# Routing an MoE layer in three groups beside the attention part, in one block, with the router on rows before the layer norm

## What is computed

```python
x = x + xattn(layernorm(x), side, ctx)      # two SmoothQuant int8 products a batch
x = x + ffn(layernorm(x), router_w, gate_proj, up_proj, down_proj)
```

## Time and profile before

| what | us |
|---|---|
| median of 3 runs (420.90 to 422.14) | 421.02 |
| profiled execution | 421.27 |
| its span, first to last instruction | 419.4 |
| PE busy | 322.5 (77%) |
| POOL busy | 246.4 (59%) |
| ACT busy | 209.7 (50%) |
| DVE busy | 209.2 (50%) |

### The profile page before, as it was taken

One profiled execution on the slowest core, in us unless ns is written; L12 is line 12 of the kernel. 1 busy time (PEld: TensorE's weight loads), 2 busy tenths in 40 slices (PEclk: granted clock), 3 DMA queues, 4 the chain that ended last, 5 costly groups with the idle time before them and its releaser, 6 DMA issues.

```text
span 419.4 us, 5809 instructions
## 1 busy us (share of the span) xinstructions
PE 322.5 (77%) x1712; PEld 202.4 (48%) x1738; DVE 209.2 (50%) x442; ACT 209.7 (50%) x378; POOL 246.4 (59%) x260
## 2 busy tenths in 40 slices
PE   0638758879887678861166999999999999999960
PEld 0525445567656446651143555555555555555530
DVE  2584899887898855500871333333333333323310
ACT  1558559878779767453101444444444444444430
POOL 2484698677869565458304265666566656656440
PEclk9957966995899795865555999999999999999996
DMA  7936406693178347035004266766666666675552
GB/s 258 314 115 216 161 41 203 192 358 100 26 253 325 109 144 275 27 125 225 1 0 127 36 117 102 131 112 115 120 125 106 116 110 125 106 134 102 90 70 27
DMA packets 26667, 57.00 MB, mean 136 GB/s; under 512 B 2576, under 2 KB 12816, under 8 KB 24592
## 3 DMA queue, kind: packets, MB, share of 16 engines
q0 software_dynamic: 8816, 20.71, 27.5%
q1 hardware_dynamic: 17824, 35.93, 24.6%
HBM read 37.50 MB, written 19.14 MB: 135 GB/s over the span
## 4 chain that ended last, share of the span: by engine, by line
issue 27%; POOL 12%; PE 8%; POOLq 2%; DMA 1%; ACT 0%; DVE 0%; SPq 0%
POOL xg L772 8%; PE bank_r L1007 4%; PE bank_h L1029 3%; POOLq L778 2%; POOL out L782 1%; DMA xg<-tokens,gather_at 1%; POOL hold_p L198 1%; POOL number L754 1%; PE bank_t L995 1%; PE bank_q L1018 0%; POOL out L757 0%; ACT y L953 0%; DVE aT L900 0%; ACT aT L948 0%; POOL no_later L764 0%
## 5 line engine op out<-in xcount | busy, mean ns | idle before, releaser
L1007 PE MATMUL bank_r<-gu_hi,xT 128*128 x312 | 107.0, 385 | 1.0 <-DVE xT L891 0.2
L782 POOL DMA_INDIRECT out<-y,scatter_at x39 | 61.7, 1583 | 51.2 <-ACT y L953 50.0
L891 DVE SCALAR_TENSOR_TENSOR xT<-bank_t,xT 128x512 f16<-128x512 f32 x39 | 27.0, 691 | 66.3 <-ACT xT L933 66.3
L772 POOL DMA_INDIRECT xg<-tokens,gather_at x39 | 38.5, 986 | 29.1 <-DVE gather_at L881 17.3
L1007 PE MATMUL bank_r<-gu_lo,xT 128*128 x144 | 55.1, 383 | 0.0
L1029 PE MATMUL bank_h<-dn_hi,aT 128*128 x156 | 52.8, 379 | 1.7 <-DVE aT L900 1.4
L953 ACT ACTIVATE y<-bank_h,slot_weight 128x512 f32<-128x512 f32 x39 | 26.8, 687 | 36.8 <-PE bank_h L1029 36.8
L1007 PEld LDWEIGHTS bank_r<-gu_hi,xT 128*128 128x128 f16 x312 | 30.8, 99 | 29.5 <-issue 2.5
L360 POOL TENSOR_TENSOR gu_lo<-stage,gu_hi 128x1024 bf16<-128x1024 f32 x16 | 34.0, 2129 | 13.1 <-ACT gu_hi L578 13.0
L933 ACT ACTIVATE xT<-bank_t 128x512 f16<-128x512 f32 x39 | 23.0, 589 | 24.8 <-PE bank_t L995 24.7
L906 DVE SCALAR_TENSOR_TENSOR gated<-bank_r,gated 128x256 f32<-128x256 f32 x39 | 16.6, 425 | 37.3 <-ACT gated L941 37.3
(11 more groups left out here) (156 smaller groups left out, 629.7 us busy)
## 6 DMA issues: line engine op xcount, KB each, us to landing
x_in<-in_x SPq DMA_DIRECT2D x4, 1024.0 KB, 5.4
w_in<-in_fside_BxS2xS SPq DMA_DIRECT2D x4, 1024.0 KB, 6.3
stage<-in_L_ffn_gate_proj SPq DMA_DIRECT2D x8, 512.0 KB, 4.9
stage<-in_L_ffn_up_proj SPq DMA_DIRECT2D x8, 512.0 KB, 3.7
stage<-in_L_ffn_down_proj SPq DMA_DIRECT2D x8, 512.0 KB, 4.8
x<-in_x SPq DMA_DIRECT2D x4, 1024.0 KB, 6.2
out<-x SPq DMA_DIRECT2D x4, 1024.0 KB, 6.7
tokens<-xn SPq DMA_DIRECT2D x4, 1024.0 KB, 6.4
```

The costliest lines, as they stand in the source:

```text
L772: pool.indirect_dma_start(out=xg[:, i % XG], out_offset=None, in_=tokens_dram, in_offset=bass.IndirectOffsetOnAxis(ap=gather_at[:, i:i + 1 ...
L782: pool.indirect_dma_start(out=out, out_offset=bass.IndirectOffsetOnAxis(ap=scatter_at[:, i:i + 1], axis=0), in_=y[:, i], in_offset=None, c ...
L891: dve.scalar_tensor_tensor(out=xT[i % 2][:, 1].rearrange("p c t -> p (c t)"), in0=bank_x[:, i % 2], scalar=X_SCALE, in1=xT[i % 2][:, 0].re ...
L1007: ins = pe.matmul(bank_gu[:, i % 2], xT[i % 2][:, part, c], rhs[:, cols], start=(c == 0 and n == 0), stop=(c == C - 1 and n == 2))
```

## The change

The second block is gone: its steps stand at the ends of the same five lists. The routing is cut in three groups, batches 0 and 1, batch 2 and batch 3. For each group there is "choose" (the two best scores, DVE), "place" (ranks on PE, then DVE gives each row a slot; each expert owns 16 tiles of 128 slots, so that a group's places don't depend on later groups), and "table" (one-hot products on PE summed into a table of 128 tiles). After the last group "list" and "indices" pick the 39 tiles in use out of the table, with five small products ("compact"). "weigh" makes the two weights on ACT from the difference of the two best scores, by a tanh. All expert tiles follow the last group (EARLY = 0). Gathers wait for the table, for all lows, and for the stored tokens of all batches.

The router reads x1, not xn2: its weight has its column mean taken off (rwc, one small instruction on DVE at the start, after four products with a constant mean on PE), and the deviation enters in place, where the gap of the two scores is multiplied by rstd. Row scales are computed for all rows of a batch in one multiply and one reciprocal. The padding row store stands at the head of SP's list, and with it the wait for POOL's zeroing. The number tables (iota, affine_select) are made by POOL at the start. Scatters count on eight semaphores; SP waits for them in turn and counts up "landed", which scatters and the y buffers (eight instead of 39) wait for. The lists of steps are reordered; before, the ends of those of POOL and DVE read "gate times up 3, low 17, root 2 3, smooth w2 3, low 18, residual 3, deviation 2 3, low 19, low 20, low 21, low 22, low 23" and "product 1 3, w2 columns 3, a columns 3, smoothing 2 3, smooth a 3, a scales 3, w2 scales 3, product 2 3, moments 2 3". In POOL's list low 12 stood before residual 1, and now low 7 does.

```diff
+EARLY = 0
...
+    "gate times up 3, deviation 2 2, low 13, low 14, root 2 3, low 15, smooth w2 3, low 16, low 17, low 18, "
+    "residual 3, low 19, deviation 2 3, low 20, low 21, low 22, low 23, gather 0")
...
+    "choose 0, product 1 3, place 0, a columns 3, table 0, smoothing 2 3, smooth a 3, a scales 3, choose 1, "
+    "w2 scales 3, place 1, product 2 3, moments 2 3, table 1, choose 2, place 2, list 0, table 2, indices 0")
...
+    "tokens 4, weigh 0, high 13, high 14, normalise 2 2, high 15, tokens 5, high 16, scores 4, rows 2 3, high 17, "
+    "scores 5, a up 3, a transposed 3, weigh 1, w2 up 3, high 18, w2 scale row 3, w2 transposed 3, high 19, tokens 6, "
+    "high 20, scores 6, tokens 7, high 21, scores 7, normalise 2 3, weigh 2, high 22, high 23")
...
+    GROUPS = [(0, 1), (2,), (3,)]
...
+            sp.wait_ge(sem("zeroed"), 1)
+            sp.dma_start(tokens_dram[N:N + P], blank).then_inc(sem("pad_stored"), 16)
...
+            sp.sem_inc(sem("landed"), 1)
+            for i in range(EARLY, TILES):
+                n = i - EARLY
+                sp.wait_ge(sem(f"added{n % (2 * J)}"), 16 * (n // (2 * J) + 1))
...
+                    pool.wait_ge(sem("pad_stored"), 16)
+                    pool.wait_ge(sem("lo_done"), 3 * E)
+                    for b in PHASES[phase][3]:
+                        pool.wait_ge(sem(f"tokens_stored{b}"), 16)
+                    pool.wait_ge(sem("gather_ready"), phase + 1)
...
+                    before = pool.value_load(scatter_after[0:1, i:i + 1], min_val=1, max_val=MOST)
+                    pool.wait_ge(sem("landed"), before)
+                    hold(pool, i)
+                    landing = sem(f"added{(i - EARLY) % (2 * J)}")
...
+                    dve.tensor_reduce(m[:, rows, 0], src[:, rows], AX.X, ALU.max, apply_absolute_value=True).then_inc(done, 1)
+                dve.wait_ge(done, upto(b, cuts + 1, cuts - 1))
+                dve.tensor_reduce(s, m, AX.X, ALU.mult).then_inc(done, 1)
+                dve.wait_ge(done, upto(b, cuts + 1))
+                dve.reciprocal(inv[:, b % 2, which, side], s).then_inc(sem(f"inv{which}{side}"), 1)
...
+                    then(dve.tensor_reduce(b, score, AX.X, ALU.max))
+                    then(dve.tensor_tensor(w, score, spread(b, shape, 3), ALU.is_equal))
+                    then(dve.tensor_tensor(w, w, liked, ALU.mult))
+                    then(dve.tensor_reduce(p, w, AX.X, ALU.max))
+                    then(dve.tensor_tensor(ch, liked, spread(p, shape, 3), ALU.is_equal))
+                    if k == 0:
+                        then(dve.scalar_tensor_tensor(out=score, in0=ch, scalar=-LEAST, in1=score, op0=ALU.mult, op1=ALU.add))
+                dve.tensor_tensor(mask[:, 0:m * J].rearrange("p (m j) e -> p m j e", j=J), chosen[:, 0:m, 0], chosen[:, 0:m, 1],
...
+            def place(g):
+
+                m, chunk = members(g)
+                dve.wait_ge(sem("shift1"), GROUPS[g][-1] + 1)
+                then(dve.tensor_tensor(gap[:, 0:m], best[:, 0, 0:m], best[:, 1, 0:m], ALU.subtract))
+                first = GROUPS[g][0] % 2
+                dve.tensor_tensor(gap[:, 0:m], gap[:, 0:m], rstd[:, first:first + m, 1], ALU.mult).then_inc(sem("gap_ready"), 1)
+                rank = ring_x.empty(dve, "place", 0, g)
+                if g > 0:
+                    ring_x.emptied(dve, "place", 0, g - 1)
+                then(dve.tensor_tensor(slot[:, 0:m].rearrange("p m (j e) -> p (m j) e", e=E),
+                                       rank[:, 0:m * J * E].rearrange("p (t e) -> p t e", e=E),
+                                       spread(base[g][:], [P, m * J, E], 1), ALU.add))
+                dve.tensor_tensor(base[g + 1][:], rank[:, m * J * E:(m * J + 1) * E], base[g][:], ALU.add).then_inc(ring_x.taken, 1)
+                then(dve.tensor_tensor(slots[:, 0:m], chosen[:, 0:m].rearrange("p m k j e -> p m k (j e)"),
+                                       spread(slot[:, 0:m], [P, m, K, J * E], 2), ALU.mult))
+                then(dve.tensor_reduce(pos[:, 0:m], slots[:, 0:m].rearrange("p m k (j e) -> p m k j e", e=E), AX.X, ALU.add))
+
+                then(dve.tensor_scalar(rounding[:, 0:m], pos[:, 0:m], 1.0 / P, 0.5 / P - 0.5, ALU.mult, ALU.add))
+                then(dve.tensor_scalar(place_of[:, 1, 0:m], rounding[:, 0:m], ROUND, ROUND, ALU.add, ALU.subtract))
+                then(dve.scalar_tensor_tensor(out=place_of[:, 0, 0:m], in0=place_of[:, 1, 0:m], scalar=-float(P), in1=pos[:, 0:m],
+                                              op0=ALU.mult, op1=ALU.add))
+
...
+                        for s in range(2):
+                            then(dve.tensor_tensor(onehot[:, k, s], number[:], spread(place_of[:, s, n, k], [P, P, J], 1), ALU.is_equal))
...
+                            dve.wait_ge(sem("weighed"), g + 1)
+                            then(dve.tensor_tensor(values[:, 2, batches], weight[:, 0:m], values[:, 1, batches], ALU.subtract))
+                        if step > 0:
+                            after_sort(step - 1)
+                        dve.tensor_tensor(packed[:], spread(onehot[:, k, 0], [P, 3, P, J], 1), spread(values[:, :, b, k], [P, 3, P, J], 2),
+                                          ALU.mult).then_inc(sem("packed"), 1)
...
+                    ins = dve.tensor_tensor(table[:], part, table[:], ALU.add)
...
+                dve.tensor_scalar(tile_onehot[:, start:start + n], tile_number[:, start:start + n], tile_at[:], valid[:, 1:2],
+                                  ALU.is_equal, ALU.mult).then_inc(sem("tiles_listed"), 1)
...
+                dve.tensor_copy(sorted_out[:, :, cols], bank[:, 0:5 * n].rearrange("p (v t) -> p v t", v=5)).then_inc(ring_w.taken, 1)
...
+                then(dve.scalar_tensor_tensor(out=unused[:, cols], in0=token, scalar=0.0, in1=pad_row[:, cols], op0=ALU.is_equal,
+                                              op1=ALU.mult))
+                then(dve.scalar_tensor_tensor(out=row_of_slot[:, cols], in0=token, scalar=-1.0, in1=unused[:, cols], op0=ALU.add,
+                                              op1=ALU.add))
+                dve.tensor_scalar(gather_at[:, cols], row_of_slot[:, cols], float(N), None, ALU.min).then_inc(sem("gather_ready"), 1)
...
+                act.wait_ge(sem("gap_ready"), g + 1)
+                act.activation(lean[:, 0:m], gap[:, 0:m], ACT.Tanh, scale=0.5).then_inc(sem("leaning"), 1)
+                act.wait_ge(sem("leaning"), g + 1)
+                for k in range(K):
+                    act.activation(weight[:, 0:m, k], lean[:, 0:m], ACT.Identity, bias=0.5 * C_SCALE,
+                                   scale=(0.5 - k) * C_SCALE).then_inc(sem("weights"), 1)
+                act.wait_ge(sem("weights"), K * (g + 1))
...
-                pe.wait_ge(sem("xn2_ready"), upto(b, J, 2 * pair + 1))
...
+                    pe.wait_ge(sem("x1_ready"), n + 1)
...
+                        ins = pe.transpose(bank[:, c * P:(c + 1) * P], x1[:, n % J, c * P:(c + 1) * P], identf[:])
...
+                for n in range(steps):
+                    step = K * GROUPS[g][0] + n
+                    pe.wait_ge(sem("packed"), step + 1)
+                    for j in range(J):
+                        ins = pe.matmul(bank[:, 0:3 * P].rearrange("p (v l) -> p v l", v=3), onehot[:, n % K, 1, :, j], packed[:, :, :, j],
+                                        start=(n == 0 and j == 0), stop=(n == steps - 1 and j == J - 1))
+                    ins.then_inc(sem("sorted") if n < steps - 1 else ring_w.filled, 1)
...
+                for v in range(3):
+                    pe.matmul(bank[:, v * n:(v + 1) * n], table[:, v], tiles, start=True, stop=True)
+                pe.matmul(bank[:, 3 * n:4 * n], expert_col[:].to_broadcast([P, P]), tiles, start=True, stop=True)
+                pe.matmul(bank[:, 4 * n:5 * n], first_col[:].to_broadcast([P, P]), tiles, start=True,
+                          stop=True).then_inc(ring_w.filled, 1)
```

More of the change, by code:

```diff
@@ new lines, in block_kernel @@
+        act_order += [("take y", TILES - 2), ("a high", TILES - 1), ("take y", TILES - 1)]
+        dve_order.append(("a low", TILES - 1))
+        pe_order += [("a low", TILES - 1), ("take y", TILES - 1)]
+        ring_t = Ring(pe_order, banks(bank_t), sem("t_filled"), sem("t_taken"),
+                      {"w1 columns": C, "x columns": C, "w2 columns": IC, "a columns": IC, "x low": 1})
+        ring_x = Ring(pe_order, [bank_r[:, 0]], sem("x_row_filled"), sem("x_row_taken"),
+                      {"rows 1": 1, "rows 2": 1, "w2 scale row": 1, "place": 1}, [("a low", 0)])
@@ new lines, in block_kernel @@
+        ring_w = Ring(pe_order, [bank_r[:, 1]], sem("w_row_filled"), sem("w_row_taken"),
+                      {"rows 1": 1, "rows 2": 1, "w1 scale row": 1, "table": 1, "indices": 1}, [("a low", 1)])
+        ring_q = Ring(pe_order, banks(bank_q), sem("q_filled"), sem("q_taken"),
+                      {"x transposed": C, "w1 transposed": C, "a transposed": IC, "w2 transposed": IC,
```

(9 more changed lines are left out.)

801 lines of the change are left out of this document (430 added, 371 removed), and 58 rows, old and new, of tables (ACT_ORDER, DVE_ORDER, PE_ORDER, POOL_ORDER).

## The result

The changed kernel takes 439.91 us (437.68 to 442.17), the kernel before 420.96; the ratio is 1.0443, 95% interval [1.0408, 1.0477]: slower by 4.4%, where 410.0 was forecast. The profiled execution is the slowest of the changed kernel's: 442.17 us, span 440.4.

The account below looks back on a forecast made before the run. Time was taken as end of batch 3, plus the routing chain to the first gather, plus a fixed PE-bound tile stage of 199.5 us. The gather coming 11.3 us earlier gave 421.3 - 11.3 = 410.0 us, range 405 to 415, with rivals 402 to 420.

Parts of the forecast that it names:

- Start and row scales: Batches 0 to 2: first load waits for POOL's zeroing, +2.1 us; 8 fewer pairs of tiny DVE instructions, -2.0 us.
- the other swaps: Remaining changes of order in the step lists: put at nothing, from -5 to +3 us.
- Place 0: First group's slots on DVE, between product 1 and a columns of batch 3: takes 10.7 us, +7.9 exposed.
- the rule against the change: Moved routing beside POOL's lows: the skill says GpSimd contends with two-SBUF-input VectorE instructions; the sum charged nothing.
- The third rival: Place 0 to 2: DVE and POOL hold each other up, eight steps and the lows take twice as long; 425, chance 0.09.
- Steps of 1.9 us: Each step of place on DVE: two one-hots of 0.42 and a packing of 0.95, with waits 1.9 us.
- Place 1 "as good as nothing": Second group's slots before product 2 of batch 3: ends at 174.5, DVE wanted at 174.2; without that cover 6.2 us.
- product 2 at 184.2: Batch 3's product 2 on DVE: starts at 184.2 us, from 171.5 + 12.7 for moved routing, start and scales.
- Product 2 to the first gather: Batch 3's router, last choose, place, list and table: from 184.2 to the gather at 208.6, before at 219.86; -11.3 us.
- The tile stage, "Nothing, from -1 to +2": First gather to end: still 199.5 us, the scatter waits' hop through SP covered by POOL's idle; -1 to +2.
- The better-packed orders: Rival: new orders use DVE's idle of the first 147 us, batch 3 late by 7, not 12.7; 404.5, chance 0.24.
- f16 with an inner run of 4 elements: Rival in place's eight steps: f16 instructions run at f32's pace, 1.3 us more a step; 420.4, chance 0.07.

Follow-up runs that it names:

- e3: Changed kernel with each of POOL's 24 subtractions replaced by two instructions that only write, leaving out the expert weights' low parts: 427.64 us.
- e15: Changed kernel with the expert-number read moved back before the down product, POOL's subtractions replaced by write-only instructions, and two buffers for packed rows: 413.74 us.
- e1: Changed kernel with TensorE's read of the next tile's expert number moved back between gate_up and the down product: 432.01 us.
- e4: Kernel before, with five POOL additions of two SBUF inputs put beside its routing on DVE: 438.32 us, ratio 1.0421.
- e13: Changed kernel with the expert-number read moved back, POOL's subtractions in pieces, one routing group per batch, place 0 behind a columns 3, two packed buffers, weigh moved: 430.47 us.
- e2: Kernel before, with only TensorE's read of the next tile's expert number moved in front of that tile's transposes: 428.56 us, ratio 1.0169.

## Why the prediction was wrong

The miss is 29.9 us. By the stretches: 0.2 in batches 0 to 2 (with the mean of 145.0), 13.1 of holds, 5.1 of sort waits, 3.8 of the rest up to the gather, 8.5 in the tile stage; together 30.7, of traces whose first mark alone scatters by 2 either way.

**Start and row scales.** DVE's first instruction came at 8.22 instead of 6.56, +1.7 for +2.1 forecast. Product 2 of batch 2, ahead of which the same steps stand in both, starts at 140.0 on the mean of the 15 kernels and at 139.4 on that of the three with before's front: +0.6 for +0.1. So the row scales and the other swaps together brought 1.1 us for the 2.0 forecast, within the scatter; no run parts the two.

**Place 0, choose 1, place 1 and the tail: the holds.** The step that failed is "by the sum that costs nothing" in the paragraph on the rule against the change. The row it was set against, lows at 2129 ns on the mean, could not speak for DVE: POOL's instruction hardly lengthens (2159), DVE's is the one that waits. The Trainium skill (GPSIMD Engine Reference, Key points) had it: GpSimd contends with VectorE instructions of two SBUF inputs. It deserved the main forecast. The third rival had the mechanism and the place, at a chance of 0.09, and the wrong price: it doubled each step, where a hold costs what is left of POOL's instruction, once for each of POOL's instructions that DVE meets. Worked out so, the 8 lows that run beside the routing in the changed trace, by up to 2.1 us, would have bounded it at 17 us; e3 measured 13.1. Its sum, 425, was also short of the other causes.

**Steps of 1.9 us.** Two one-hots and a packing are 1.8, as forecast. The term left out is the wait for PE's sort between packings, 0.9 to 1.7 us each: 4.0 us ahead of product 2 and 1.1 behind it, and e15 got back 5.0. I had charged the last sort only. The reason was in the code, one buffer. The low clock, to which the sum put its estimate of 1.4 us for a sort, is not the reason. Windows of the changed kernel over place 0's first and second sort:

```profile
163.00:164.60 1.60, 1.52 (x4) 0.38 (x4) 1.57 (x2) 1.57 (x3) 1.60 (x1) 1.00 0.00 0
168.40:170.00 1.60, 1.54 (x4) 0.40 (x4) 0.70 (x2) 0.00 (x0) 0.00 (x0) 0.50 0.83 289
```

The sort takes 1.52 us at a granted clock of 1.00 and 1.54 at 0.50. What sets its length no run here shows.

**Place 1 "as good as nothing", product 2 at 184.2.** It came at 200.2. With holds and sort waits gone (e15) the stretch is 41.4 for 39.4 forecast. The sum had no term for rows 2 3 behind scores 4 (DVE waited 2.8 us there, 1.0 before), which would be 1.8 of the 2.0; the rest is the balance of smaller misses, such as place 0, charged 0.8 too much.

**Product 2 to the first gather.** 24.4 forecast, 32.3 measured, 26.2 with both causes gone. The order of its steps was right, and the gather was released by DVE's gather_at, as written; POOL's last low and the store did not show. The 1.8 us that e15 leaves over the forecast stay without a cause here.

**The tile stage, "Nothing, from -1 to +2".** I counted the hop of the scatter waits, which was right (e1), and overlooked that the read of the expert number changed its place in PE's order. PE bounds this stage by itself, so a move of 0.2 us there, 38 times, is 8 us: the read should have been a term of its own.

**The rivals.** The better-packed orders did not show (product 2 of batch 2 came 0.6 us later, not sooner), and f16 with an inner run of 4 elements keeps its pace: 0.42 and 0.96 us. The range, 402 to 420, had only the causes of which I had a price.

## What to carry to other kernels

Before moving VectorE work beside GpSimd work, list which instructions of each have two SBUF inputs, and charge one remaining GpSimd instruction for each meeting; if it doesn't fit, give GpSimd's subtraction to VectorE, which does it in 1.22 us instead of 2.13, inside its own waits. With a single buffer between VectorE and TensorE, charge VectorE's wait for each step and not for the last alone: 0.9 to 1.7 us here, by sorts of 1.53 us at either clock. In a stage bound by TensorE's own queue, the place of a scalar read counts for each tile.

## What the runs showed of the hardware

- A VectorE instruction with two SBUF inputs that meets a two-input GpSimd instruction lasts until that one ends, whatever its size: 0.29 us of work took 3.65 beside additions of 3.7 us (e4), 128x64 elements took 2.07 (changed kernel). Reductions, batch statistics and write-only GpSimd instructions (e3) stood outside of it. But a single input is not always safe: `rounding`, 128x16 float32 in and out, took 0.88 instead of 0.17 beside GpSimd's product at 159.09, and again in e15.
- It works the other way too: GpSimd's `shift`, begun at 162.24 beside a packing that ran until 162.93, took 0.75 us instead of 0.20. GpSimd loses less because VectorE's instructions here are short: a subtraction between them took 2.31 instead of 2.13; in e13's pieces of 0.64 us some groups of four took 3.73 instead of 2.56.
- TensorE's read of a register from SBUF shows as "issue" in front of the loads for the transposes: 0.56 us at the tile shown of the changed kernel, 0.20 to 0.69 at e2's tiles from 250 to 303 us; the tile stages say 0.2 us a tile. Ahead of the down product's weights 0.21 us stands with the read (e1) and without it (changed kernel, e2): there it costs nothing.
